# A two-layer decoder block on one Trainium2 core: fewer decay sums, and the routed network and the last memory's first half begun within the routing

## The reference, cut to what matters

```python
# layer 0, mixer: a state-space model with 16 heads, state 128
A_cumsum = cumsum(dA); L = exp(segsum(dA))
Y_diag = einsum(C, B, L, x); states = einsum(B, exp(A_cumsum[-1] - A_cumsum), x)
Y_off = einsum(C, decayed states, exp(A_cumsum)); x = x + out_proj(y * silu(z))
# memory cross attention
x = x + softmax(u @ ctx.T / sqrt(512), masked) @ ctx
# routed network, for each sequence of 512 rows
w = u @ W_r + b_r; vals, idx = top_k(w, 128); xg = u[idx]
h = gelu(xg @ W1 + b1)                 # 512 -> 2048
blk = h @ W2 + b2                      # 2048 -> 512
out = zeros.at[idx].add(blk * w[idx] * (w[idx] > threshold)) + u * (w <= threshold)
# layer 1: 16-head attention, a cross product with the memory in 8 bits (each
# 128x128 block of ctx scaled, rounded to fp8 and scaled back), a ternary network
```

## Time and profile before

| | us |
|---|---|
| median of 3 runs | 1101.39 (1101.0 to 1102.41) |
| the profiled execution's own time | 1102.29 |
| its span in the trace | 1100.6 |
| busy PE, DVE, ACT, POOL | 1050.0, 846.6, 639.5, 480.3 |
| mean granted clock of PE, of full speed | 0.998 |

### The profile page before, as it was taken

How to read it: one execution, slowest core, us unless ns; L and a number is a source line. 1 busy time by engine, 2 the same in 40 slices (tenths; PEclk the granted TensorE clock), 3 DMA queues, 4 the chain that set the end, 5 groups by cost and what they waited for, 6 DMA issues and landing times.

```text
span 1100.6 us, 15542 instructions
## 1 busy us (share of the span) xinstructions
PE 1050.0 (95%) x5255; PEld 785.1 (71%) x5255; DVE 846.6 (77%) x1612; ACT 639.5 (58%) x1243; POOL 480.3 (44%) x727
## 2 busy tenths in 40 slices
PE   7999999999999999999999999998899999999898
PEld 6777888788878888766566777776676666666544
DVE  6787766776677767846988758858888988978975
ACT  5643444344444443336566547663468889888784
POOL 8343324332433323425888513205654554644520
PEclk9999999999999999999999999999999999999999
DMA  8300000000000000217010035420001211212122
GB/s 292 113 1 1 1 1 1 1 1 1 1 1 1 1 1 1 80 47 301 34 39 1 1 129 185 151 93 1 1 6 24 34 37 33 51 33 51 33 55 75
DMA packets 46446, 52.48 MB, mean 48 GB/s; under 512 B 32544, under 2 KB 33568, under 8 KB 44064
## 3 DMA queue, kind: packets, MB, share of 16 engines
q1 hardware_dynamic: 46368, 51.49, 14.8%
HBM read 39.92 MB, written 4.19 MB: 40 GB/s over the span
## 4 chain that ended last, share of the span: by engine, by line
PE 59%; DVE 17%; POOL 11%; issue 6%; ACT 6%; DMA 1%; POOLq 0%; DVEq 0%; ACTq 0%
PE bank L422 44%; PE bank L520 3%; PE bank L430 3%; PE bank L870 3%; DVE cum_h L992 1%; PE bank L511 1%; PE bank L531 1%; DVE half_lo L1362 1%; DVE prod L1484 1%; POOL wq L2492 1%; PE bank L781 1%; PE bank L501 1%; POOL wq L2488 1%; DVE wgt L1000 1%; DVE y L1028 1%
## 5 line engine op out<-in xcount | busy, mean ns | idle before, releaser
L422 PE MATMUL bank<-win_hi,a_uT_hi 128*128 128x512 f32 (+1 forms) x320 | 126.0, 394 | 5.8 <-DVE win_lo L943 3.1
L422 PE MATMUL bank<-win_lo,a_uT_hi 128*128 128x512 f32 (+1 forms) x320 | 119.7, 374 | 0.0
L422 PE MATMUL bank<-win_hi,a_uT_lo 128*128 128x512 f32 (+1 forms) x320 | 119.4, 373 | 0.0
L1761 ACT ACTIVATE ex<-bank 128x48 f32<-128x48 f32 x16 | 3.4, 210 | 144.5 <-PE bank L475 144.5
L2356 POOL TENSOR_TENSOR y<-y,off 128x512 f32<-128x512 f32 x24 | 38.1, 1587 | 106.1 <-DVE off L1013 106.1
L422 PEld LDWEIGHTS bank<-win_hi,a_uT_hi 128*128 128x128 f32 x320 | 60.3, 188 | 19.5 <-issue 3.9
L422 PEld LDWEIGHTS bank<-win_lo,a_uT_hi 128*128 128x128 f32 x320 | 60.3, 188 | 12.4 <-issue 2.4
L422 PEld LDWEIGHTS bank<-win_hi,a_uT_lo 128*128 128x128 f32 x320 | 60.2, 188 | 11.3
L520 PEld LDWEIGHTS bank<-xs,wgt 128*128 128x128 f32 x512 | 61.1, 192 | 7.7 <-issue 5.7
L422 PE MATMUL bank<-wq,eT 128*128 128x512 f32 x128 | 58.8, 602 | 6.5 <-ACT eT L2095 6.5
L422 PE MATMUL bank<-f,fqT_next 128*128 128x512 fp8e4 (+1 forms) x312 | 64.0, 362 | 0.0
(11 more groups left out here) (358 smaller groups left out, 3203.2 us busy)
## 6 DMA issues: line engine op xcount, KB each, us to landing
wchunk<-w_in SPq DMA_DIRECT2D x32, 256.0 KB, 4.8
stage<-f_in SPq DMA_DIRECT2D x4, 1408.0 KB, 6.6
x<-x_in SPq DMA_DIRECT2D x16, 256.0 KB, 6.2
land<-win_in SPq DMA_DIRECT2D x4, 1024.0 KB, 8.8
wq<-ctxT_in SPq DMA_DIRECT2D x4, 1024.0 KB, 6.2
out<-x SPq DMA_DIRECT2D x16, 256.0 KB, 2.0
ctx<-ctx_in SPq DMA_DIRECT2D x3, 1024.0 KB, 4.8
first_stage<-f_in SPq DMA_DIRECT2D x2, 1408.0 KB, 14.2
```

The costliest lines, as they stand in the source:

```text
L422: made = e.matmul(bank, a, b, start=start and n == 0, stop=stop and n == len(pairs) - 1)
```

## The change

- The mixer makes only the sums that a tile needs: the first tile of a sequence the one beyond a row, the middle tiles two, the last the one up to a row. The sum over the tile is no longer made; POOL multiplies ex[0] by ex[1] instead (`whole_decay`), for the middle tiles.
- The routing counts directly in PSUM, without `keep_row`. The choice is stored as bf16, the running additions are gone, and the positions are four bf16 products. The count starts at 1, which saves the subtraction of 1.
- The routed network's first two steps of up, for the first three sequences (384 columns), go into the routing loop of PE (`early_up`), with their gelu for step 0 and its part of down; the last sequence's 128 columns follow after its gather (`late_up`). The weight halves are made two loop steps earlier.
- The last memory's first half is quantised in the last steps of the routing loop; its second half follows, with the DVE part in step 5 of the network.
- The dummy products of the last sequence go from 19, 19 and 5 to 3, 5 and 0, with 7 ahead of early_up(0). The second half of the last stage of ternary weights is loaded after chunk 13, not 14; small shifts of `keep_x` and `sum_abs` follow.

```diff
@@ -470,10 +489,10 @@
     w.wait_ge("mixer_consts", 1)
     w.wait_ge("dt_step", 7 * m + 4)
     logs = dt[m % 2][:, 2, :]
-    e.matmul(bank[:, 0:NH], upto_r[:].bitcast(F32), logs, start=True, stop=True)
-    e.matmul(bank[:, NH:2 * NH], beyond[:], logs, start=True, stop=True)
-    e.matmul(bank[:, 2 * NH:3 * NH], ones[:].broadcast_to([P, P]), logs, start=True, stop=True).then_inc(
-        sig("sums_done"), 1)
+    for n in sums_of(m):
+        made = e.matmul(bank[:, n * NH:(n + 1) * NH], (upto_r[:].bitcast(F32), beyond[:])[n], logs, start=True,
+                        stop=True)
+    made.then_inc(sig("sums_done"), 1)
 def running(i):
...
@@ -660,9 +679,9 @@
     b, c = divmod(n, TPB)
     if c < TPB - 1:
         return
-    bank = banks.claim(w, ("row", b), "route_kept", 3 * b + 1)
+    bank = banks.claim(w, ("row", b), "route_step", 3 * b + 1)
     if b == BATCH - 1:
-        keep_busy(bank, 19)
+        keep_busy(bank, 3)
...
@@ -673,21 +692,21 @@
     b, c = divmod(n, TPB)
     if c < TPB - 1:
         return
-    bank = banks.claim(w, ("pos", b), "route_step", 7 * b + 6)
-    w.wait_ge("consts", 10)
-    keep_busy(bank, 19 if b == BATCH - 1 else 3)
-    w.wait_ge("route_step", 7 * b + 5)
-    e.matmul(bank[:, 0:TPB], before[:], route[b][:, 4, :], start=True, stop=False)
-    e.matmul(bank[:, 0:TPB], ones[:].broadcast_to([P, P]), route[b][:, 5, :], start=False, stop=True).then_inc(
-        sig("route_turn"), 1)
+    bank = banks.claim(w, ("pos", b), "route_step", 3 * b + 3)
+    keep_busy(bank, 5 if b == BATCH - 1 else 3)
+    w.wait_ge("route_step", 3 * b + 2)
+    sel = selected(b)
+    made = e.matmul(bank[:, 0:TPB], before_b[:], sel, start=True, stop=False)
+    for c in range(1, TPB):
+        made = e.matmul(bank[:, c:TPB], ones_b[:].broadcast_to([P, P]), sel[:, 0:TPB - c], start=False,
+                        stop=c == TPB - 1)
+    made.then_inc(sig("route_turn"), 1)
 def gather(n):
     b, c = divmod(n, TPB)
     if c < TPB - 1:
...
+def early_up(f):
+    bank = banks.claim(w, ("early", f), "hT_hi", f + 1)
+    if f == 0:
+        keep_busy(bank, 7)
+    w.wait_ge("gathered_lo", BATCH - 1)
+    w.wait_ge("half_lo_0", f + 1)
+    hi, lo = half_hi[0][f % 2], half_lo[0][f % 2]
+    pairs = []
+    for k in range(KD):
+        cols = slice(k * P, (k + 1) * P)
+        pairs += thrice(hi[:, cols], lo[:, cols], gathered_hi[:, k, first_slots], gathered_lo[:, k, first_slots])
+    product(bank[:, first_slots], pairs).then_inc(sig("early_up"), 1)
+def late_up(f):
+    bank = banks.of["early", f]
+    hi, lo = half_hi[0][f % 2], half_lo[0][f % 2]
+    tiles = [slice(k * P, (k + 1) * P) for k in range(KD)]
+    w.wait_ge("route_kept", 2 * BATCH - 1)
+    product(bank[:, last_slots], [(half[:, tiles[k]], gathered_hi[:, k, last_slots])
+                                  for k in range(KD) for half in (hi, lo)], stop=False)
+    w.wait_ge("gathered_lo", BATCH)
+    product(bank[:, last_slots], [(hi[:, tiles[k]], gathered_lo[:, k, last_slots]) for k in range(KD)],
+            start=False).then_inc(sig("up_done"), 1)
+def down_part(f, b):
+    slots = slice(b * SLOTS, (b + 1) * SLOTS)
+    return product(accs[b][:], thrice(hT_hi[f % 2][:, slots], hT_lo[f % 2][:, slots],
+                                      half_hi[1][f % 2][:], half_lo[1][f % 2][:]),
+                   start=f == 0, stop=f == KF - 1)
+def early_down(b):
+    w.wait_ge("early_h_lo", 1)
+    w.wait_ge("half_lo_1", 1)
+    down_part(0, b)
 scores(1)
 turn_p(0)
@@ -718,22 +773,32 @@
...
     if t1 is not None and t1 > 2:
         scores(t1)
+    if n == NT + 3:
+        early_up(0)
     if t4 is not None:
         spread_weights(t4)
+    if n == NT + 4:
+        early_up(1)
+        accs = [banks.claim(w, ("acc", b), "blk_ready", b + 1) for b in range(BATCH)]
+        banks.set_aside([k for k in range(8) if banks.banks[k] in accs])
     if t2 is not None:
         spread_tops(t2)
     if t0 is not None:
         turn_u(t0)
+    if n == NT + 5:
+        early_down(0)
+        early_down(1)
     if t6 is not None:
         gather(t6)
     if t5 is not None:
         positions(t5)
-accs = [banks.claim(w, ("acc", b), "blk_ready", b + 1) for b in range(BATCH)]
-banks.use([n for n in range(8) if banks.banks[n] not in accs])
+early_down(2)
...
@@ -1037,7 +1099,7 @@
     if m % TPB in (0, TPB - 1):
         return
     oi, _ = order_of(m)
-    w.wait_ge("ex_ready", m + 1)
+    w.wait_ge("y_off", 2 * oi + 2)
     w.wait_ge("state_ready", 2 * oi + 2)
     w.wait_ge("off_done", 2 * oi + 2)
     e.tensor_tensor(by_head(state[:]), by_head(state[:]), heads(ex[m % 2][:, 2, :], 0, NH),
...
@@ -1272,37 +1334,29 @@
     b, c = divmod(n, TPB)
     if c < TPB - 1:
         return
-    wc, cnt, sel, acc = (route[b][:, n, :] for n in range(2, 6))
-    w.wait_ge("route_kept", 3 * b + 1)
+    wc, cnt = (route[b][:, n, :] for n in (2, 3))
+    w.wait_ge("route_turn", 4 * b + 1)
     w.wait_ge("weighed", b + 1)
     w.wait_ge("vector_step", dotted[-1])
     for c in range(TPB):
-        made = e.tensor_scalar(spare[:], wrow[:], wc[:, c:c + 1], None, ALU.is_ge, ALU.add,
+        made = e.tensor_scalar(spare[:], banks.of["row", b][:], wc[:, c:c + 1], None, ALU.is_ge, ALU.add,
                                accum_out=cnt[:, c:c + 1])
         if c < TPB - 1:
             made.then_inc(sig("vector_step"), 1)
             w.wait_ge("vector_step", own.next())
     made.then_inc(sig("route_step"), 1)
-    w.wait_ge("route_step", 7 * b + 1)
-    e.memset(acc[:, 0:1], 0.0)
-    e.tensor_scalar(sel, cnt, SLOTS - 0.5, None, ALU.is_lt).then_inc(sig("route_step"), 1)
-    for c in range(1, TPB):
-        w.wait_ge("route_step", 7 * b + 1 + c)
-        e.tensor_tensor(acc[:, c:c + 1], acc[:, c - 1:c], sel[:, c - 1:c], ALU.add).then_inc(
-            sig("route_step"), 1)
+    w.wait_ge("route_step", 3 * b + 1)
+    e.tensor_scalar(selected(b), cnt, SLOTS - 0.5, None, ALU.is_lt).then_inc(sig("route_step"), 1)
 def pick_slots(n):
     b, c = divmod(n, TPB)
     if c < TPB - 1:
         return
-    r = route[b]
-    sel, pos = r[:, 4, :], r[:, 6, :]
+    pos = route[b][:, 6, :]
     w.wait_ge("route_turn", 4 * b + 2)
-    e.scalar_tensor_tensor(out=pos, in0=banks.of["pos", b][:, 0:TPB], scalar=1.0, in1=sel, op0=ALU.add,
-                           op1=ALU.mult).then_inc(sig("route_step"), 1)
-    w.wait_ge("route_step", 7 * b + 6)
-    e.tensor_scalar(pos, pos, -1.0, None, ALU.add).then_inc(sig("route_step"), 1)
-    w.wait_ge("route_step", 7 * b + 7)
+    e.scalar_tensor_tensor(out=pos, in0=banks.of["pos", b][:, 0:TPB], scalar=1.0, in1=selected(b),
+                           op0=ALU.add, op1=ALU.mult).then_inc(sig("route_step"), 1)
+    w.wait_ge("route_step", 3 * b + 3)
     w.wait_ge("consts", 11)
     if b:
         w.wait_ge("route_turn", 4 * b)
...
         quantise(t2, 0)
     if n == NT + 4:
-        low_half(0, 0)
+        w.wait_ge("early_h", 1)
+        low_h_part(first_slots, "early_h_lo")
     if t5 is not None:
         pick_slots(t5)
+    if n == NT + 4:
+        memory_magic(BATCH - 1, 0)
     if t2 is not None:
         memory_scales(t2)
     if t0 is not None and t0 > 0:
         memory_limits(t0)
-    if n == NT + 4:
-        low_half(0, 1)
     if t4 is not None:
         select(t4)
     if t7 is not None:
         low_gathered(t7)
     if t2 is not None:
         invert_sum(t2)
-    if n == NT + 4:
+    if n == NT + 2:
+        low_half(0, 0)
+        low_half(0, 1)
         low_half(1, 0)
     if t3 is not None:
         weigh(t3)
...
@@ -1446,15 +1514,17 @@
 for f in range(KF):
     low_h(f)
+    if f == 0:
+        low_half(0, 2)
     if f + 1 < KF:
         low_half(1, f + 1)
-    if f + 2 < KF:
+    if f and f + 2 < KF:
         low_half(0, f + 2)
-    if f in (4, 6):
-        memory_magic(BATCH - 1, f // 2 - 2)
-    if f in (0, 7, 14):
-        ternary_scale((0, 7, 14).index(f))
-    for n, first in enumerate((0, 7, 14)):
+    if f == 5:
+        memory_magic(BATCH - 1, 1)
+    if f in (1, 7, 14):
+        ternary_scale((1, 7, 14).index(f))
+    for n, first in enumerate((1, 7, 14)):
...
-        w.wait_ge("state_decayed", decay_count(m - 2))
         w.wait_ge("off_scaled", 2 * off_count(m - 2))
         w.wait_ge("xs_weighted", state_count(m - 2))
-    e.activation(ex[m % 2][:].rearrange("p a h -> p (a h)"), banks.of["sums", m][:, 0:3 * NH],
+    cols = slice(sums_of(m)[0] * NH, (sums_of(m)[-1] + 1) * NH)
+    e.activation(ex[m % 2][:].rearrange("p a h -> p (a h)")[:, cols], banks.of["sums", m][:, cols],
                  ACT.Exp).then_inc(sig("ex_ready"), 1)
 def high_cum(i):
...
@@ -2009,22 +2080,23 @@
         square_u(3)
     if t2 is not None and t2 > 1:
         exp_scores(t2)
-    if n == NT + 4:
-        high_half(0, 0)
+    if n == NT + 3:
+        high_half(0, 1)
+        high_half(1, 0)
     if t4 is not None:
         normal_v(t4)
-    if n == NT + 4:
-        high_half(0, 1)
+    if n == NT + 3:
+        early_gelu()
     if t7 is not None:
```

(31 more changed lines are left out.)

88 lines of the change are left out of this document (56 added, 32 removed).

## The result

The changed kernel takes 1095.62 us in the median of 4 runs (1093.51 to 1096.69), the kernel before 1101.90 in the same comparison: ratio 0.9941, 95% interval 0.9924 to 0.9959. The forecast was 1091.8 in 1087 to 1096. The gain is 6.3 us where 9.6 were forecast (1101.4 to 1091.8), and its interval is clear of none. So the sign and the range held, and the time stands 3.8 us above the forecast one.

What follows compares the result with a forecast made beforehand. It took TensorE (PE) to bound the kernel. Its terms, -3.6 -1.2 +1.1 -5.7 +0.3 -1.0 +0.6 = -9.5, took the profiled 1102.3 us to 1092.8; with the median 0.9 lower it forecast 1091.8, range 1087 to 1096.

Steps and rivals of the forecast that it cites:

- Fewer sums: Mixer: 24 of 48 fp32 decay-sum products go, won only where PE isn't made to wait afterwards; -3.6 us, range -5.5 to 0.
- rival E: Mixer: the saving turns into waits all through, PE being only last in a ring of engines; +3.6 us, chance 0.07.
- Batches 0 to 2: Routing of the first three batches: running additions go and positions products get cheaper; -1.2 us, range -2 to 0.
- The tail up to the gather: Last tile's routing: -1.1 from steps removed, +2.2 from moved steps colliding; gather ends +1.1 us later.
- +2.2 for the two: Routing tail: low_half delays POOL's deviation and scale_up collides with weigh; last weight +2.2 us later, range 0 to 3.
- Gather's end to up(2): Head of the routed network: 10.93 us becomes 5.2, most of up being done early; -5.7 us, range -6.5 to -2.7.
- rival D: Network's head: late_up's small products cost what large ones do, or ACT bounds it; +3.0 us, chance 0.08.
- Rest of the network: Routed network after up(2): POOL's scale_up(3,1) meets a DVE step, +0.3 us; both waits for hT_lo go, -1.0 us.
- The first scatter: Network's end: scatter(0) takes batch 3's bank, so its 1.48 us wait on blk grows by one addition; +0.6 us.
- rival C: Routing tail: the collision makes PE wait and its granted clock falls; +1.6 us, chance 0.15.
- the signs that it named: Signs of being right included a mixer stage 3 to 4 us shorter and the last weigh at 2 us or more.
- rival F: Head of the network: PE's low clock for some 24 us of work makes it slower than before, about 1103.8 us; chance 0.03.

Runs made afterwards that it cites:

- e4: The kernel before with only the fewer decay sums and the whole decay on POOL: 1101.94 us against 1101.45, ratio 1.0006.
- e1: The changed kernel with the first scatter dealt a PSUM bank that no accumulator of the routed network holds: 1094.14 us, ratio 0.9941.
- e2: The changed kernel with the first scatter dealt the bank of batch 2's accumulator, as in the kernel before: 1095.12 us, ratio 0.9943.
- e5: The changed kernel with the last memory's first half put back behind the routing loop, both halves there: 1097.80 us, ratio 0.9959.
- e10: The changed kernel with e6's edit, dummies at the mixer's end, low_half(0,1) and (1,0) behind the last weights, scale_up and half of wqkv_lo later: 1090.89 us, ratio 0.9884.
- e7: The changed kernel with an early-free bank for the last tile's pair product and two low_halfs behind weigh, ahead of weights_done: 1096.85 us, ratio 0.9939.
- e9: The kernel before with e6's edit and dummy products in three waits at the mixer's end: 1102.69 us against 1103.82, ratio 0.9988.
- e6: The changed kernel with e1's bank and dummy products in four waits of layer 1 that had none: 1093.47 us, ratio 0.9910.

## Why the prediction was right, and where it was off

- **Fewer sums, -3.6: mis-sized.** It measured -1.6 over the tiles 0 to 11 and -1.8 with tile 12, and e4 shows the same. The forecast left out the third tile of a sequence, where PE waits for un, and rightly: that wait grew from 0.81 to 1.03. But it counted two products saved in each last tile, 0.45 us each time in three sequences, and these went into a wait for un of 0.28 that had not been there; rival E held for half of the term. Another 1.1 came between the mixer's end and the attention, not from the sums: the stretch at half clock fell at 461 instead of 471, where it cost 1.2. That was luck.
- **Batches 0 to 2, -1.2:** -1.4 in the changed kernel and five of the runs with its routing, -1.9 in e1 and e2. Right.
- **The tail up to the gather, +1.1:** +0.1. The mechanism held: deviation +0.6, weigh +0.8 where I had +2.2 for the two. weigh became ready 0.92 us after scale_up's start, when ACT's normal_v of 0.82 us was done, and not 0.5, so that it lost only the last part of scale_up's 1.89. The other side was right (-1.3 against -1.1). The Trainium skill's rule on interference ("SBUF — State Buffer", who interferes with whom) named the pair; e5 and e10, with the pair apart, show 0.69, and the trace agrees with it. The 62 cycles that the Trainium skill gives for a PSUM source ("VectorE: DVE Perf Modes", the TRN2 errata) are not seen: 0.75 us either way.
- **Gather's end to up(2), -5.7:** 10.93 to 4.90, -6.0. Right, rival D out: late_up's products were 0.11 us apart. The steps that the forecast lists add up to 4.9 us and not to its 5.2.
- **Rest of the network, +0.3 -1.0:** -0.6. Right in size; of the waits for hT_lo the one at 722 stayed (0.56 us at 711) and the other went.
- **The first scatter, +0.6:** right. Its wait grew from 1.48 to 2.12, and where the clock stayed up (e5, e7) that made layer 1 start 0.6 later. A bank freer than the old one would win nothing (e1), since DVE's wqkv_lo comes last then.
- **The clock, left at +1.6 as rival C:** the chance of 0.15 was for the tail; there the clock stayed at 1.00. It fell in layer 1, in the wait of the earlier trace rows and three others that the change does not touch, and cost 1.7, 1.3 and 1.5 us: with the bank's 0.6 these make up the 5.0 given back, within rounding. I had read those waits as harmless because one profile showed 1.00 there. One execution says how long a wait is, and not whether the clock falls behind it.

Up to blk the forecast is -10.1 and the measured gain 10.8 us; so far the misses, among them 1.8 on the sums, 1.0 on the tail and the lucky 1.1, cancel. Of the signs that it named two were missed: the attention starts 2.9 us sooner, not 3 to 4, and weigh took 1.52 us, not 2 or more. Two slips of its arithmetic change little: 1102.3 less 9.5 and 0.9 is 1091.9, and in rival F the 12 us are lost over 24 us of time at the low level, not over 24 us of work. Behind blk the forecast had no term for the clock. It had been built on a profile of the kernel before with a single stretch. The execution of the changed kernel with one stretch (clock 0.998) took 1091.93 us, those of the kernel before with one, in the same comparison, 1102.61 to 1102.86: 10.7 or more apart, which fits the 10 us from e9 and e10.

The changed kernel has more stretches on average: a mean clock of 0.9939 over its ten executions, 0.9956 over the fifty of the kernel before in the comparisons of e1 to e10, by the count above 3.9 against 2.8. Within the one comparison that has both (six executions against twelve, 0.9940 against 0.9957) the difference isn't clear of noise. Why it should have more stays open; the two longer waits (2.06 against 1.6 us at the mixer's end, 2.12 against 1.48 at the scatter) may be part of it, which no run shows.

## What to carry to other kernels

Read the waits of the slowest engine in stages that a change doesn't touch: each is a place where the granted clock may fall in some executions, and they can take back part of a saving made upstream. Count the stretches in every execution by its mean clock before comparing two profiles. A saving in a tile loop counts only where no wait stands behind it; ask for that wait, and for slack that is nearly used up, before multiplying by the number of tiles. When a run sets out to show that a wait isn't on the path, see that it differs from its parent in that wait alone: e2 had the full clock too. Before moving an elementwise step of POOL, look at which two-operand instruction of DVE it will stand beside: the same half memory's steps cost 0.8 us beside weigh, 0.3 at most beside the counts, and 5.6, a stretch at half clock included, beside the ternary weights' steps in the network.

## What the runs showed of the hardware

- A fall of the granted clock takes PE to half for some 3.4 us and then ends (0.66 over 5 us, in ten windows above); twice two came in direct succession (0.57 over 8 us, in e6 and e1). Behind the same wait it comes in some executions and not in others: 6 of 9 behind 2.13 us, 1 of 9 behind 2.05.
- It costs 1.2 to 1.7 us on the path, or nothing where PE waits again soon after (the one at 751).
- DVE's instructions with a single tensor input suffered beside POOL too: a TENSOR_SCALAR over 1408 columns took 2.98 us beside POOL's round_add, 0.89 alone.
